# Attention layer: values' bias through the projection, copies of v on ScalarE, the bias add in another step

## What is computed

```python
x = x + _L0_attn_ref(_layernorm(x), ...)
x = x + _L0_ffn_ref(_layernorm(x), ...)
x = x + _L1_attn_ref(_layernorm(x), Wq, bq, Wk, bk, Wv, bv, Wp, bp)
x = x + _L1_ffn_ref(_layernorm(x), W1, W2, Wg, bg)

def _L1_attn_ref(x, Wq, bq, Wk, bk, Wv, bv, Wp, bp):
    q, k, v = proj(Wq, bq), proj(Wk, bk), proj(Wv, bv)        # 16 heads of 16
    energy = where(|i - j| > 128, fmin, q k^T)
    att = softmax(energy / sqrt(256))
    return (att v) Wp^T + bp

def _L1_ffn_ref(x, W1, W2, Wg, bg):
    logits = xf @ Wg + bg                                     # the expert is its argmax
```

## Time and profile before

| | |
|---|---|
| time, 3 runs | median 1394.51 us (1394.25 to 1395.08) |
| profiled execution | 1400.14 us, its span 1398.1 us |
| TensorE busy | 1336.1 us (96%) |
| VectorE busy | 688.0 us (49%) |
| ScalarE busy | 489.1 us (35%) |
| GpSimd busy | 448.3 us (32%) |
| mean granted TensorE clock | 0.988 of full |

### The profile page before, as it was taken

One profiled execution on the slowest core, in us unless ns is written; L12 is line 12 of the kernel. 1 busy time (PEld: TensorE's weight loads), 2 busy tenths in 40 slices (PEclk: granted clock), 3 DMA queues, 4 the chain that ended last, 5 costly groups with the idle time before them and its releaser, 6 DMA issues.

```text
span 1398.1 us, 25005 instructions
## 1 busy us (share of the span) xinstructions
PE 1336.1 (96%) x8348; PEld 1036.2 (74%) x8348; DVE 688.0 (49%) x2499; ACT 489.1 (35%) x1046; POOL 448.3 (32%) x541
## 2 busy tenths in 40 slices
PE   7899999999999999999999999999998999999998
PEld 5566556688998998656666666666666788999998
DVE  5655457233333333337878888888887231310000
ACT  2221211122222222113666666666755412111111
POOL 2100000253222221242454454544323524343332
PEclk9999999999999999998999999999999999999999
DMA  9402011067777777243554554645442779999996
GB/s 327 129 31 72 4 41 43 22 220 234 234 243 238 237 236 226 67 120 100 143 155 140 148 154 130 181 116 150 146 128 75 273 289 312 346 333 344 332 347 210
DMA packets 95676, 254.29 MB, mean 182 GB/s; under 512 B 12189, under 2 KB 42271, under 8 KB 85568
## 3 DMA queue, kind: packets, MB, share of 16 engines
q1 hardware_dynamic: 79728, 217.61, 47.8%
q0 software_dynamic: 12096, 32.13, 7.4%
q10 hardware_dynamic: 3728, 2.97, 0.7%
HBM read 201.42 MB, written 52.17 MB: 181 GB/s over the span
## 4 chain that ended last, share of the span: by engine, by line
PE 84%; DVE 8%; issue 4%; ACT 2%; DMA 0%; DVEq 0%; ACTq 0%; POOLq 0%
PE psum L994 10%; PE psum L1004 10%; PE psum L675 10%; PE psum L813 10%; PE psum L796 7%; PE psum L686 6%; PE psum L851 4%; PE psum L898 4%; PE psum L873 4%; PE psum L922 3%; DVE work L1892 3%; PE psum L823 2%; PE psum L956 2%; PE psum L768 2%; PE psum L933 2%
## 5 line engine op out<-in xcount | busy, mean ns | idle before, releaser
L1892 DVE CUSTOM_DVE_ANT_0 work<-psum,mask 128x384 bf16<-128x384 f32 (+1 forms) x512 | 230.6, 485 | 59.3 <-PE psum L851 57.6
L851 PE MATMUL psum<-kz,qT 96*128 96x384 f32 (+1 forms) x512 | 167.3, 398 | 10.6 <-DVE small L1892 9.5
L1971 POOL DMA_INDIRECT work<-normed,token_of x71 | 67.5, 951 | 325.1 <-PE psum L768 198.2
L813 PEld LDWEIGHTS psum<-work,arena 128*128 128x128 f32 x1136 | 136.1, 193 | 15.7 <-ACT work L1148 11.0
L675 PE MATMUL psum<-arena 128*128 128x512 f32 x320 | 147.7, 600 | 0.0
L813 PE MATMUL psum<-work,arena 128*128 128x128 f32 x1136 | 143.6, 280 | 4.0 <-ACT work L1148 2.2
L994 PEld LDWEIGHTS psum<-arena 128*128 128x128 f32 x1248 | 145.5, 192 | 2.4 <-issue 0.4
L994 PE MATMUL psum<-arena 128*128 128x128 f32 x1248 | 146.2, 275 | 0.0
L1244 ACT ACTIVATE arena<-psum 128x384 f32<-128x384 f32 x256 | 112.2, 494 | 93.7 <-PE psum L873 92.8
L1004 PE MATMUL psum<-arena 128*128 128x256 f32 x624 | 143.1, 383 | 0.5 <-issue 0.5
L1746 DVE TENSOR_TENSOR arena<-psum,arena 128x256 f32<-128x256 f32 x39 | 16.6, 425 | 245.8 <-PE psum L1004 245.8
(11 more groups left out here) (243 smaller groups left out, 1993.0 us busy)
## 6 DMA issues: line engine op xcount, KB each, us to landing
arena<-in_w SPq DMA_DIRECT2D x78, 1024.0 KB
arena<-in_wgu SPq DMA_DIRECT2D x71, 704.0 KB, 5.0
strips<-hi SPq DMA_DIRECT2D x64, 256.0 KB
kz<-strips SPq DMA_DIRECT2D x64, 192.0 KB, 3.1
qT<-strips SPq DMA_DIRECT2D x32, 384.0 KB, 4.6
results<-work SPq DMA_DIRECT2D x71, 128.0 KB
strips<-lo SPq DMA_DIRECT2D x32, 256.0 KB
normed<-work SPq DMA_DIRECT2D x14, 512.0 KB, 3.1
```

Of the source, the lines that this page charges most:

```text
L813: m = e.matmul(psum[:, b % 2, q * P:(q + 1) * P], wu0[:, b % 4, c, q * P:(q + 1) * P], xsT0[:, b % 2, c * P:(c + 1) * P], start=(c == 0), ...
L851: m = e.matmul(psum[:, bk, at:at + w], qT[0:ROWS_S, slot, half, i * P:(i + 1) * P], kz[slot][0:ROWS_S, hd, lo_key:hi_key], start=True, sto ...
L1892: e.tensor_tensor_reduce(masked[:, n % 2, 0:w], psum[:, bank_of["scores", u, i, hd], at:at + w], mask[:, P - off:P - off + w], 1.0, MASKED ...
L1971: e.indirect_dma_start(out=xs[:, b % 3, :], out_offset=None, in_=normed[l][0:n, :], in_offset=bass.IndirectOffsetOnAxis(ap=token_of[:, l, ...
```

## The change

- The biases bv (values) and bp (projection) are joined: a new product pe_bias_proj in step LEAD + 2 of the mix multiplies bv, spread over 128 columns, with w_p including its gate columns; dve_bias_proj adds it to b_p, which has 264 columns now. bp's own product with the gate goes there too. w_p is loaded at the start, on ScalarE's queue, in place of bv's broadcast; SP's later load of w_p goes.
- dve_v is removed. act_v, on ScalarE, in the same step, between the two halves of the exponentials, copies v without a bias and the gate columns scaled by std.
- GpSimd's bias add covers all 264 columns and is done in step 14 of its own batch instead of step -12; it waits for all of the batch's v copies.

```diff
@@ pe_gate_proj
-            e.wait_ge(wb_loaded, 16 * 2)
+            e.wait_ge(wb_loaded, 16 * 3)
...
+        def pe_bias_proj(e, ring):
+            bk = next_of(ring)
+            fill(e, ("bias_proj",), bk)
+            e.wait_ge(bp_spread, 2)
+            e.wait_ge(wp_made, 1)
+            for c in range(EC):
+                m = e.matmul(psum[:, bk, 0:XW], bp_wide[:, c, :], w_p[:, c, :], start=(c == 0), stop=(c == EC - 1))
+            m.then_inc(bank_full[bk], 1)
@@ pe_mix
                 if s == LEAD + 1:
                     pe_gate_proj(e, ring)
+                if s == LEAD + 2:
+                    pe_bias_proj(e, ring)
@@ pe_residual
                 if b == 0:
-                    e.wait_ge(wp_made, 1)
+                    e.wait_ge(bias_made, 1)
@@ act_mix
-            e.dma_start(bp_raw, a["bpT"]).then_inc(wb_loaded, 16)
-            for dst, n, w in ((b_v, "bv", E), (b_p, "bp", E), (b_gate, "bg", NX)):
-                e.dma_start(dst[:, :], a[n].rearrange("(o n) -> o n", o=1).broadcast_to([P, w])).then_inc(bias_loaded, 16)
+            e.dma_start(bp_raw, a["bpvT"]).then_inc(wb_loaded, 16)
+            e.dma_start(w_p[:, :, 0:E], a["wpT"].rearrange("(c p) n -> p c n", p=P)).then_inc(wb_loaded, 16)
+            for dst, n, w in ((b_p, "bp", E), (b_gate, "bg", NX)):
+                e.dma_start(dst[:, 0:w], a[n].rearrange("(o n) -> o n", o=1).broadcast_to([P, w])).then_inc(bias_loaded, 16)
@@ act_attention
                     act_turned(e, 2, b, xnT[:, b % 2, 0, :])
+                for b, t in v_due(s - 1):
+                    act_v(e, b, t)
...
+        def act_v(e, b, t):
+            if t == 0:
+                e.wait_ge(pads_made, 1)
+                e.wait_ge(std_made, b + 1)
+                if b >= 2:
+                    e.wait_ge(*done["values", NG * (b - 2) + NG - 1])
+            e.wait_ge(*done["v", b, t])
+            i = b * TPB + t
+            e.activation(X[:, i, E:XW], psum[:, bank_of["v", b, t], E:XW], ACT.Copy, scale=std[:, i:i + 1])
+            e.activation(v32[:, b % 2, t, :, 0:DH], heads(psum[:, bank_of["v", b, t], 0:E]), ACT.Copy).then_inc(v_made, 1)
@@ setup on VectorE
-        def dve_spread_bias(e):
-            e.wait_ge(wb_loaded, 16 * 2)
-            e.wait_ge(masks_zeroed, 1)
+        def dve_spread_bias(e, i):
             for c in range(EC):
-                m = e.tensor_scalar(bp_wide[:, c, :], ones[:, :], bp_raw[:, c:c + 1], None, ALU.mult)
+                m = e.tensor_scalar(bp_wide[:, c, :], ones[:, :], bp_raw[:, i, c:c + 1], None, ALU.mult)
             m.then_inc(bp_spread, 1)
...
-            e.tensor_copy(bp_gate[:, :], got[:, EC, :])
+            e.tensor_copy(b_p[:, E:XW], got[:, EC, :])
             e.tensor_copy(w_p[:, :, E:XW], got[:, 0:EC, :]).then_inc(wp_made, 1)
+            dve_spread_bias(e, 1)
+
+        def dve_bias_proj(e):
+            e.wait_ge(bias_loaded, 16 * 3)
+            e.wait_ge(wp_made, 1)
+            e.wait_ge(*done["bias_proj",])
+            e.tensor_tensor(b_p[:, :], b_p[:, :], psum[:, bank_of["bias_proj",], 0:XW], ALU.add).then_inc(bias_made, 1)
@@ dve_attention
-                for b, t in v_due(s - 1):
-                    dve_v(e, b, t)
@@ dve_v, removed
-            e.scalar_tensor_tensor(X[:, i, E:XW], psum[:, bank_of["v", b, t], E:XW], std[:, i:i + 1], bp_gate[:, :],
-                                   ALU.mult, ALU.add)
-            e.tensor_tensor(v32[:, b % 2, t, :, 0:DH], heads(psum[:, bank_of["v", b, t], 0:E]), heads(b_v[:, :]),
-                            ALU.add).then_inc(v_made, 1)
@@ pool_attention
-                for b, _ in batch(s, -12):
+                for b, _ in batch(s, 14):
                     t0 = b * TPB
                     e.wait_ge(xn_made, NORMED[2, b] + 1)
+                    e.wait_ge(v_made, TPB * (b + 1))
                     if b == 0:
-                        e.wait_ge(bias_loaded, 16 * 4)
-                    e.tensor_tensor(X[:, t0:t0 + TPB, 0:E], X[:, t0:t0 + TPB, 0:E],
-                                    b_p[:, :].rearrange("p (o c) -> p o c", o=1).broadcast_to([P, TPB, E]),
+                        e.wait_ge(bias_made, 1)
+                    e.tensor_tensor(X[:, t0:t0 + TPB, :], X[:, t0:t0 + TPB, :],
+                                    b_p[:, :].rearrange("p (o c) -> p o c", o=1).broadcast_to([P, TPB, XW]),
                                     ALU.add).then_inc(bias_added, 1)
@@ sp_mix
-            e.dma_start(w_p[:, :, 0:E], a["wpT"].rearrange("(c p) n -> p c n", p=P)).then_inc(wc_loaded, 16)
```

More of the change, by code:

```diff
@@ L234, in build @@
         std = sb("std", [P, NT])
-        bp_gate = sb("bp_gate", [P, NX])
         b_gate = sb("b_gate", [P, NX])
         b_qk = sb("b_qk", [P, 2, EC])
-        b_v = sb("b_v", [P, E])
-        b_p = sb("b_p", [P, E])
+        b_p = sb("b_p", [P, XW])
         stats = sb("stats", [P, 2 * TPB, 6])
@@ L291, in build @@
         ew_sb = carve(work, 3528, 2, XW)
-        bp_raw = carve(work, 4056, EC)
+        bp_raw = carve(work, 4056, 2, EC)
         wp_raw = carve(arena, 29952, EC, E)
@@ L369, in build @@
         xT_loaded = [sem(f"xT_loaded{b}") for b in range(B)]
-        centred, wo_made, wb_loaded, bp_spread, wp_made, v_gate_made, std_made = (
-            sem(n) for n in ("centred", "wo_made", "wb_loaded", "bp_spread", "wp_made", "v_gate_made", "std_made"))
+        centred, wo_made, wb_loaded, bp_spread, wp_made, bias_made, v_gate_made, std_made = (
+            sem(n) for n in ("centred", "wo_made", "wb_loaded", "bp_spread", "wp_made", "bias_made", "v_gate_made", "std_made"))
         wa_loaded, bias_loaded, wd0_loaded, sh_loaded, wc_loaded = (
@@ L426, in emptied @@
                 return wp_made, 1
+            if kind == "bias_proj":
+                return bias_made, 1
             if kind == "kv":
@@ L917, in pe_qk @@
                     if b == 0:
-                        e.wait_ge(wc_loaded, 16 * 2)
+                        e.wait_ge(wc_loaded, 16)
                 fill(e, ("qk", b, c, i), next_of(ring))
@@ L1371, in dve_mix @@
                 if s == LEAD:
-                    dve_spread_bias(e)
+                    e.wait_ge(wb_loaded, 16 * 3)
+                    e.wait_ge(masks_zeroed, 1)
+                    dve_spread_bias(e, 0)
                 if s == LEAD + 1:
                     dve_gate_proj(e)
+                if s == LEAD + 2:
+                    dve_bias_proj(e)
                 for b in due(s, 7):
@@ L2233 @@
         "wqkvT": np.concatenate([g["L1_attn_Wq"], g["L1_attn_Wk"], g["L1_attn_Wv"]]).T,
-        "bqkT": np.concatenate([g["L1_attn_bk"], g["L1_attn_bq"]]).reshape(-1, P).T, "bv": g["L1_attn_bv"],
-        "wpT": g["L1_attn_Wp"].T, "wp": g["L1_attn_Wp"], "bp": g["L1_attn_bp"], "bpT": g["L1_attn_bp"].reshape(EC, P).T,
+        "bqkT": np.concatenate([g["L1_attn_bk"], g["L1_attn_bq"]]).reshape(-1, P).T,
+        "wpT": g["L1_attn_Wp"].T, "wp": g["L1_attn_Wp"], "bp": g["L1_attn_bp"], "bpvT": np.stack([g["L1_attn_bp"], g["L1_attn_bv"]]).reshape(2, EC, P).transpose(2, 0, 1),
         "w1": g["L1_ffn_W1"].reshape(NX, EC, P, HID).transpose(0, 2, 1, 3).reshape(NX, P, EC * HID),
```

1 line of the change is left out of this document (removed).

## The result

The changed kernel takes 1.0042 times the time before, with a 95% interval of 1.0028 to 1.0056: medians of five runs each are 1401.34 us (1399.29 to 1402.39) and 1394.51 us (1393.33 to 1397.48). On the median of before this is 5.9 us more, 1400.4 us. The profiled execution took 1402.39 us, its span is 1400.6.

The account below looks back on a forecast made before the run. It took TensorE as the bound in mid-attention (busy 390.8 of 420 us), so relieving VectorE gives at most some 29 us. Terms -6.5 + 6.5 + 2.3 - 1.0 + 0 + 0.9 + 0.2 = +2.4 gave 1396.9 us; range 1390.3 to 1400.8.

Parts of the forecast that it names:

- rival B: Steps 5 and 6 of every batch: ScalarE becomes the bound, 0.5 us each in 8 batches, 1400.9 us; chance 0.15.
- rival D: Steps 14 and 126: meetings cost 0.4 us more each, TensorE falling to its lower clock, 1399.5 us; chance 0.08.
- The add leaves step 4: Step 4 modulo 16, batches 3 to 7: bias add no longer holds L1904; five meetings gone, -6.5 us.
- It meets L1859 in step 14: Step 14, batches 1 to 5: GpSimd's add holds L1859 and delays the values' product; five meetings, +6.5 us.
- Rival A: Step 14: two-input instructions as long as L1859 are not held by the add, 1390.4 us; chance 0.20.
- the count of five: Step 14: meetings only in batches 1 to 5, 1.3 us each; in batch 0 L1859 comes before the add.
- The last add: Step 126: batch 7's add holds the token list's L1736 or the cast behind it, +2.3 us.
- v's copies leave VectorE: Step 9 chain: VectorE loses copies L1872 and L1874; 0.15 us gained for each of 7, -1.0 us.
- rival C: Steps 5 and 9: VectorE's relief is worth more, 0.4 us in each of 15, 1391.9 us; chance 0.12.
- They arrive on ScalarE: Between a step's two exponentials: v's copies take 0.6 us per tile, set with VectorE's relief in step 5 at 0.
- The setup: Start of the kernel: one more product of two matmuls, +0.9 us, and larger first loads, +0.2 us.
- The +0.2 for the loads: First loads: 128 KB more net, 0.4 us at 327 GB/s, half of it covered, +0.2 us.

Follow-up runs that it names:

- e2: Changed kernel with the bias add in step 18 of its batch instead of 14; ratio to the kernel before 0.9978.
- e3: Kernel before with only the bias add (256 columns) moved from step -12 to step 18 of its batch; ratio to the kernel before 0.9963.
- e9: Changed kernel with the bias add of step 14 as four GpSimd instructions of one tile each; ratio to the kernel before 0.9976.
- e5: Changed kernel with only the last batch's bias add moved from step 126 to 130; ratio to the kernel before 1.0003.
- e1: Kernel before with only the bias add moved from step -12 to step 14 of its batch; ratio to the kernel before 1.0032.
- e7: Changed kernel without the product of bv with the projection and its add to the bias; ratio to the kernel before 1.0027.
- e4: Changed kernel with the bias add back in step -12 on 256 columns; v's copies on ScalarE and bias product stay; ratio to the kernel before 1.0013.
- e8: Changed kernel with the fetched tile of step 14 added by VectorE in step 13, with that step's own; ratio to the kernel before 1.0026.
- e10: Kernel before with its bias add still in step -12 but as four GpSimd instructions of one tile; ratio to the kernel before 0.9974.
- e11: Changed kernel with the bias add in step 18 and without the product of bv and its add; ratio to the kernel before 0.9950.
- e12: Kernel before with the bias add in step 18 and as four instructions of one tile; ratio to the kernel before 0.9973.

## Why the prediction was right or wrong

The forecast was 1396.9 us, the outcome 1400.4, inside the range and on the side (slower) that had the largest chance, 0.41 against 0.40 for no change. Both are in part luck. The forecast itself lay within what I called no change, and the upper end of the range was the value of rival B (given as 1400.8, worked out as 1400.9), whose mechanism did not appear (point 5); without B the range would have ended at D's 1399.5, below the outcome (and D's 0.4 us for each of six meetings is 2.4, not the 2.6 used). The main mechanism was right; the change was more than twice the forecast's. Point by point:

1. *The add leaves step 4:* right. -6.5 forecast, -6.7 seen; L1904 (now L1922) is no longer at 1.7 us.
2. *It meets L1859 in step 14:* right, and shown: +6.5 forecast, +5.8 in the same five stretches, gone in e2, e3 and e9. Rival A falls. What I took from the Trainium skill (SBUF — State Buffer, Who interferes with whom), that such a pair contends and the one that starts first keeps the ports to its end, agrees with the 2.20 us here and with e9, where VectorE gets in after one piece and the add takes 0.24 us more; batch 0 does not fit it as recorded. The step that failed is the count of five: "in step 14 of batch 0 it comes before the add". It does, and is held all the same:

```profile
681.43 0.95 POOL L2015 DMA_INDIRECT arena<-results,slot_of  x1
681.70 0.08 DVE L1910 DVE_READ_ACCUMULATOR2_ANT small<- 128x1 f32 x1
681.70 3.44 DVE L1892 SCALAR_TENSOR_TENSOR X<-arena,top_w,X 128x256 f32<-128x256 f32 x1
682.41 2.44 POOL L2049 TENSOR_TENSOR X<-X,b_p 128x1056 f32<-128x1056 f32 x1
...
686.27 0.96 PE L910 MATMUL psum<-arena 128*32 128x256 f32 x12 [1.18 <-DVE work L1936]
```

   L1892 is recorded 0.7 us before the add and still ends only at 685.14, 0.3 us after it: a sixth meeting. The gather in progress does not hold it by itself. In e2, with the same gather and no add behind it, it takes 0.48 us and ends within the gather:

```profile
681.51 0.95 POOL L2015 DMA_INDIRECT arena<-results,slot_of  x1
...
681.79 0.48 DVE L1892 SCALAR_TENSOR_TENSOR X<-arena,top_w,X 128x256 f32<-128x256 f32 x1
```

   So it takes the add queued behind the gather, though by its 0.48 us L1892 would have ended 0.23 us before the add's recorded start. Why is open.

   What this meeting costs depends on the clock. Where the granted clock stays full in this stretch it is **1.2** us: 14.74 and 14.78 in after and e5, 13.50 and 13.48 in e9 and e3. In the other nine kernels the clock falls within it (a mean of 0.79 to 0.89), and there the stretch is 14.76 and 14.84 with the meeting (e1, e7) and 14.70 to 16.18 without it (before, e2, e4, e8, e10, e11, e12): the meeting adds nothing that can be seen, and against before's profile, 15.19, it isn't a loss at all. Before, then e3, from 675 to 685 us:

```profile
675.00:680.00 5.00, 4.27 (x18) 3.05 (x18) 4.60 (x18) 3.84 (x8) 3.88 (x6) 0.87 0.63 175
680.00:685.00 5.00, 5.00 (x27) 3.16 (x29) 3.55 (x15) 1.50 (x3) 1.39 (x3) 0.78 0.97 208
```

```profile
675.00:680.00 5.00, 4.28 (x22) 3.27 (x23) 4.63 (x19) 3.47 (x7) 3.88 (x7) 1.00 0.55 141
680.00:685.00 5.00, 5.00 (x45) 2.41 (x44) 3.55 (x16) 1.88 (x3) 1.12 (x2) 1.00 1.05 237
```

3. *The last add:* the mechanism was right, L1736 (now L1771) held for 2.27 us; +2.3 forecast, +2.6 against before. Against the same kernel without the meeting (e5) it is 3.9, since the clock falls behind the wait. That is the mechanism of rival D, about 1.5 us once, at step 126, but before's clock fell there too, so it adds nothing against before's profile. In the five meetings of step 14 no clock fell, in any kernel that has them.
4. *v's copies leave VectorE:* -1.0 forecast. e2 against e3, which differ by the copies and the setup: four stretches from 3 to 7 are 0.12 shorter each, 31 to 35 is 0.2 shorter, 35 to 39 0.3 longer, 115 to 119 0.4 shorter; -0.8 in all. Right; rival C falls.
5. *They arrive on ScalarE:* right at 0. From 811 to 821 us ScalarE is busy 8.45 us against 8.41 before, and TensorE's matmuls wait 2.6 us in all for the first exponentials, against 2.7 before. Rival B falls.
6. *The setup:* this term was mis-sized, 1.1 us forecast and 1.8 to 3.5 found. +0.9 for the product was its matmuls alone. "VectorE's four small instructions lie beside it" failed for one of them, L1377, which frees the bank: 1.30 us in place, 0.51 more in steps 15 to 19, and the 1.7 us of the clock where it falls. The +0.2 for the loads can't be seen: the first matmul starts at 8.62 us against 8.67 before.

The terms as the stretches give them: -6.7 + 5.8 + 2.6 - 0.6 (the part of point 4 outside the stretches of point 1) + 1.8 = +2.9. The sixth meeting adds 1.2 where the clock is full in batch 0 and nothing where it falls; the fall of the clock at 210 us adds 1.7 where it comes with the change. That makes +2.9 to +5.8; measured +5.9 (3.9 to 7.8). So my +2.4 was short for certain by 0.7 in the setup; that the sixth meeting and the clock make up the rest fits, but how often the clock is full or falls in before's and after's executions isn't known from one profile of each, and it is not shown. The two profiled spans differ by 2.5 us only (1398.1 and 1400.6). e1 and e3 against their own sums leave 1 to 3 us over as well; before's profiled execution was 5.6 us above its median, and a comparison of single stretches with it is good for the causes and not for the last 2 us.

## What to carry to other kernels

Two engines that hold each other, as GpSimd and VectorE do here, must be scheduled as pairs: find the longest instruction on one, list what the other starts under it, and move it to a step where nothing on the path does; or cut it in pieces, so that one instruction that is met costs at most the rest of one piece (the next instruction can meet the next piece, as in step 126 of e9). Moving the other engine's instruction is no cure where that engine has no slack in the step that receives it. And a small product put into the setup costs more than its matmuls: here 0.90 us for them and 0.40 more, as the next matmuls wait until another engine has read its bank.

## What the runs showed of the hardware

- A GpSimd instruction that is cut in four takes longer, 2.87 us where it meets nothing instead of 2.45, and gives VectorE 1.6 us back: L1892 in step 30 takes 0.57 instead of 2.20 us.
- The hold reaches a tensor_scalar with one SBUF input: L1922 is held to 1.71 us in e4, L1771 to 2.27 in the changed kernel, just as the scalar_tensor_tensor with two inputs is.
- The lower clock can't be told from TensorE's stops alone: the same stop of 2.3 us at 207 us led to it in eight profiles of thirteen, and around 676 us, where TensorE's longest wait was 0.57 us in before and 0.52 in e3 and its busy time equal, the clock fell in before (0.87, then 0.78) and stayed full in e3. One kernel's runs spread with it: e12's twelve runs go from 1388.92 us at a mean granted clock of 0.993 to 1398.67 at 0.985. Differences of 0.2% need a dozen runs, and the stretches of a trace then tell what the median can't.
